# Attention loop of a sandwich layer: a third probability buffer, semaphores per pair of exps, and P·V moved three tiles behind Q·K

## What is computed

```python
q = (x @ Wq + bq).reshape(b, t, H, hd).transpose(0, 2, 1, 3)          # H = 16 heads of 64
k = ((x @ Wk + bk) @ Wl + bl).reshape(b, t, H, lhd).transpose(0, 2, 1, 3)
v = ((x @ Wv + bv) @ Wl + bl).reshape(b, t, H, lhd).transpose(0, 2, 1, 3)
attn = softmax(einsum('bhqd,bhkd->bhqk', q, k) / sqrt(hd))
out = einsum('bhqk,bhkd->bhqd', attn, v)
```

## Time and profile before

| | us |
|---|---|
| median of 2 runs | 4394.33 (4388.55 to 4400.11) |
| the profiled execution | 4391.0 |
| its span on the slowest core (core 2) | 4389.4 |
| spans of all cores | 4366.3 to 4389.4 |
| PE busy, mean granted clock | 2287.8 (52%), 0.762 |
| DVE busy | 1556.0 (35%) |
| ACT busy | 1307.2 (30%) |

### The profile page before, as it was taken

One profiled execution on the slowest core, in us unless ns is written; L12 is line 12 of the kernel. 1 busy time (PEld: TensorE's weight loads), 2 busy tenths in 40 slices (PEclk: granted clock), 3 DMA queues, 4 the chain that ended last, 5 costly groups with the idle time before them and its releaser, 6 DMA issues.

```text
span 4389.4 us, 33357 instructions; the slowest of 8 cores (4366.3 to 4389.4 us)
## 1 busy us (share of the span) xinstructions
PE 2287.8 (52%) x9208; PEld 781.5 (18%) x9296; DVE 1556.0 (35%) x2228; ACT 1307.2 (30%) x1117; POOL 10.1 (0%) x16
## 2 busy tenths in 40 slices
PE   3777555655555554777655555556553333233333
PEld 1333111111111111333211111111111121111121
DVE  2444222232223223444222322222232544555445
ACT  0000355554554550000255454555551000000000
POOL 0000000000000000000000000000000000000000
PEclk9888777877777776888877777778776665566666
DMA  6000100000000002000100000000003112222121
GB/s 116 20 20 1 20 0 0 20 0 20 1 0 20 0 0 77 20 20 1 20 1 1 20 0 0 20 0 20 1 0 82 60 75 96 96 96 88 67 95 58
DMA packets 52842, 137.04 MB, mean 31 GB/s; under 512 B 7479, under 2 KB 7614, under 8 KB 52670
## 3 DMA queue, kind: packets, MB, share of 16 engines
q1 hardware_dynamic: 42206, 117.59, 7.7%
q0 software_dynamic: 10464, 17.32, 2.7%
HBM read 101.87 MB, written 50.33 MB: 35 GB/s over the span
## 4 chain that ended last, share of the span: by engine, by line
PE 34%; DVE 26%; ACT 23%; issue 8%; DMA 5%; DVEq 3%; ACTq 1%; SPq 1%; another core or an unknown queue 0%; POOL 0%; POOLq 0%
ACT pt_sb L434 22%; PE ps L323 13%; DVE xn_fm L468 10%; PE ps L448 3%; PE ps L853 3%; PE ps L508 3%; PE ps L474 3%; PE ps L451 2%; DMA xst<-z_scr 2%; DVEq L165 2%; PE ps L417 1%; DVE xn_tok L487 1%; DVE xn_fm L465 1%; DVE u_s L489 1%; DVE k_sb L885 1%
## 5 line engine op out<-in xcount | busy, mean ns | idle before, releaser
L434 ACT ACTIVATE pt_sb<-ps,cst_sb 128x1024 bf16<-128x1024 f32 x512 | 616.1, 1203 | 984.4 <-PE ps L421 911.1
L448 PE MATMUL ps<-pt_sb,vt_sb 128*65 128x512 bf16 x1024 | 437.0, 427 | 516.1 <-ACTq L165 429.6
L434 ACT ACTIVATE pt_sb<-psT,cst_sb 128x1024 bf16<-128x1024 f32 x512 | 616.1, 1203 | 121.7 <-issue 95.9
L465 DVE COPY xn_fm<-ps 1x512 f32<-1x512 f32 x64 | 43.8, 685 | 1511.1 <-PE ps L451 1511.1
L451 PE MATMUL ps<-pt_sb,vt_sb 128*65 128x512 bf16 x1024 | 437.6, 427 | 0.0
L468 DVE RECIPROCAL xn_fm<-xn_fm 1x1024 f32<-1x1024 f32 x64 | 418.6, 6541 | 5.1
L474 PE MATMUL ps<-xn_fm,ones_sb 1*64 1x512 f32 x128 | 123.8, 1068 | 524.2 <-DVEq L165 524.2
L323 PE MATMUL ps<-xn_fm,arena 128*128 128x512 bf16 x1504 | 349.6, 392 | 30.1 <-DMA blrow_bf<-blrow 15.6
L448 PEld LDWEIGHTS ps<-pt_sb,vt_sb 128*65 128x65 bf16 x1024 | 115.5, 113 | 869.3 <-issue 869.3
L417 PE MATMUL ps<-q_sb,k_sb 64*128 64x512 bf16 x512 | 232.1, 453 | 45.3 <-DMA arena<-wo 38.3
L421 PE MATMUL ps<-q_sb,k_sb 64*128 64x512 bf16 x512 | 232.3, 454 | 0.0
(11 more groups left out here) (137 smaller groups left out, 2214.7 us busy)
## 6 DMA issues: line engine op xcount, KB each, us to landing
xst<-x SPq DMA_DIRECT2D x32, 512.0 KB, 7.6
z_scr<-xst SPq DMA_DIRECT2D x64, 256.0 KB, 3.9
xst<-z_scr SPq DMA_DIRECT2D x64, 256.0 KB, 6.0
k_sb<-x SPq DMA_DIRECT2D x32, 512.0 KB, 8.4
x_scr<-q_sb SPq DMA_DIRECT2D x32, 512.0 KB, 2.6
k_sb<-x_scr SPq DMA_DIRECT2D x32, 512.0 KB, 5.5
out<-q_sb SPq DMA_DIRECT2D x32, 512.0 KB, 2.9
arena<-wq POOLq DMA_DIRECT2D x2, 2048.0 KB, 23.1
```

The lines of the kernel that those rows point to most:

```text
L434: return sc.activation(ptflat[:, pk, :], stb[pk][:, 0:1024], AF.Exp, bias=cst[:, 1:2], scale=cst[:, 0:1])
L448: t.matmul(avA[0:65, :], vt_sb[:, tkc, j, 0:65], pt_sb[:, pk, 0, :], start=(tkc == 0), stop=(tkc == 15))
```

## The change

`pt_sb` gets a third buffer, and exp(t) writes buffer t mod 3, so that it waits for AV(t-3) in place of AV(t-2). ACT's semaphore is raised only after odd exps; whatever waits for exp(t) with t even and is appended after exp(t+1) waits for the value of exp(t+1). AV(t) is appended three tiles behind QK, and ahead of QK(t+3). The two copies of the sums become one of 1 x 1024.

```diff
-        pt_sb = sb("pt_sb", [128, 2, 2, SLT], BF16)
+        pt_sb = sb("pt_sb", [128, 3, 2, SLT], BF16)
...
                     def emit_qk(tkc):
                         pk = tkc % 2
-                        we = exp_done.get((j, tkc - 2)) if tkc >= 2 else \
-                            exp_done.get((j - 1, 14 + tkc) if j > 0 else (7, 14 + tkc))
+                        pp = tkc % 3
+                        wk_ = (j, tkc - 2) if tkc >= 2 else \
+                            ((j - 1, 14 + tkc) if j > 0 else (7, 14 + tkc))
+                        we = exp_done.get(wk_)
+                        if we is None and wk_ in exp_done:
+                            we = exp_done.get((wk_[0], wk_[1] + 1))
...
-                        wav = av_done.get((j, tkc - 2)) if tkc >= 2 else \
-                            av_done.get((j - 1, 14 + tkc) if j > 0 else (7, 14 + tkc))
-                        def fexp(sc, tkc=tkc, pk=pk, qk=qk_done, wav=wav):
+                        wav = av_done.get((j, tkc - 3)) if tkc >= 3 else \
+                            av_done.get((j - 1, 13 + tkc) if j > 0 else (7, 13 + tkc))
+                        def fexp(sc, tkc=tkc, pk=pk, pp=pp, qk=qk_done, wav=wav):
...
-                        exp_done[(j, tkc)] = inc("S", sS)
+                        if tkc % 2 == 1 or tkc == 15:
+                            exp_done[(j, tkc)] = inc("S", sS)
+                            exp_done[(j, tkc - 1)] = exp_done[(j, tkc)]
+                        else:
+                            exp_done[(j, tkc)] = None
...
                     def emit_av(tkc):
-                        pk = tkc % 2
+                        pp = tkc % 3
+                        ed = exp_done[(j, tkc)] or exp_done.get((j, tkc + 1))
...
-                    for tkc in range(17):
+                    AVLAG = 3
+                    for tkc in range(16 + AVLAG):
+                        if tkc >= AVLAG:
+                            emit_av(tkc - AVLAG)
                         if tkc < 16:
                             emit_qk(tkc)
-                        if tkc >= 1:
-                            emit_av(tkc - 1)
...
-                        v.tensor_copy(den_sb[0:1, 0:512], avA[64:65, :])
-                        v.tensor_copy(den_sb[0:1, 512:1024], avB[64:65, :])
+                        v.tensor_copy(den_sb[0:1, :], av2[64:65, :])
```

More of the change, by code:

```diff
@@ L101, in build_nc @@
         vt_sb = sb("vt_sb", [128, 16, 8, 130], BF16)
-        pt_sb = sb("pt_sb", [128, 2, 2, SLT], BF16)
-        pth = pt_sb.bitcast(F32).reshape([128, 1024])
+        pt_sb = sb("pt_sb", [128, 3, 2, SLT], BF16)
+        pth = pt_sb.bitcast(F32).reshape([128, 1536])
         dummy = pth[:, 0:1024]
@@ L138, in build_nc @@
         xn3_tok = ur[:, 2048:4096].rearrange("p (t d) -> p t d", t=2)
-        hs_brhs = pt_sb.reshape([128, 2048])[:, 0:SLT]
+        hs_brhs = pt_sb.reshape([128, 3072])[:, 0:SLT]
         lg_sb = xth[0:6, 0:512]
@@ L393, in emit_phase_B @@
             stb = [ps1[:, 0:1024], psTf[:, 0:1024]]
-            avb = [ps2[:, 0:512], ps2[:, 512:1024]]
+            av2 = ps2[:, 0:1024]
             drb = [ps2[:, 1024:1536], ps2[:, 1536:2048]]
-            ptflat = pt_sb.reshape([128, 2, 1024])
+            ptflat = pt_sb.reshape([128, 3, 1024])
             exp_done = {}
@@ L404, in emit_phase_B @@
                     par = j % 2
-                    avA, avB = avb
+                    avA, avB = av2[:, 0:512], av2[:, 512:1024]
                     def emit_qk(tkc):
                         pk = tkc % 2
-                        we = exp_done.get((j, tkc - 2)) if tkc >= 2 else \
-                            exp_done.get((j - 1, 14 + tkc) if j > 0 else (7, 14 + tkc))
+                        pp = tkc % 3
[4 more added lines that the diff above has]
+                            we = exp_done.get((wk_[0], wk_[1] + 1))
                         def fqk(t, j=j, tkc=tkc, qb=qb, pk=pk, we=we,
@@ L433, in fexp @@
                                 sc.wait_ge(sT.h, wav)
-                            return sc.activation(ptflat[:, pk, :], stb[pk][:, 0:1024],
+                            return sc.activation(ptflat[:, pp, :], stb[pk][:, 0:1024],
                                                  AF.Exp, bias=cst[:, 1:2],
@@ L437, in emit_qk, with fav @@
                         Q["S"].append(fexp)
-                        exp_done[(j, tkc)] = inc("S", sS)
+                        if tkc % 2 == 1 or tkc == 15:
[3 more added lines that the diff above has]
+                            exp_done[(j, tkc)] = None
                     def emit_av(tkc):
-                        pk = tkc % 2
+                        pp = tkc % 3
+                        ed = exp_done[(j, tkc)] or exp_done.get((j, tkc + 1))
                         wat = attn_done.get(j - 1 if j >= 1 else 7)
-                        def fav(t, j=j, tkc=tkc, pk=pk, ed=exp_done[(j, tkc)],
+                        def fav(t, j=j, tkc=tkc, pp=pp, ed=ed,
                                 avA=avA, avB=avB, wat=wat):
@@ L448, in fav @@
                             t.matmul(avA[0:65, :], vt_sb[:, tkc, j, 0:65],
-                                     pt_sb[:, pk, 0, :],
+                                     pt_sb[:, pp, 0, :],
                                      start=(tkc == 0), stop=(tkc == 15))
                             return t.matmul(avB[0:65, :], vt_sb[:, tkc, j, 65:130],
-                                            pt_sb[:, pk, 1, :],
+                                            pt_sb[:, pp, 1, :],
                                             start=(tkc == 0), stop=(tkc == 15))
@@ L455, in emit_av, with fden @@
                         av_done[(j, tkc)] = inc("T", sT)
-                    for tkc in range(17):
+                    AVLAG = 3
+                    for tkc in range(16 + AVLAG):
+                        if tkc >= AVLAG:
+                            emit_av(tkc - AVLAG)
                         if tkc < 16:
                             emit_qk(tkc)
-                        if tkc >= 1:
-                            emit_av(tkc - 1)
-                    def fden(v, avA=avA, avB=avB, ad=av_done[(j, 15)]):
+                    def fden(v, av2=av2, ad=av_done[(j, 15)]):
                         v.wait_ge(sT.h, ad)
-                        v.tensor_copy(den_sb[0:1, 0:512], avA[64:65, :])
-                        v.tensor_copy(den_sb[0:1, 512:1024], avB[64:65, :])
+                        v.tensor_copy(den_sb[0:1, :], av2[64:65, :])
                         v.drain()
```

## The result

The changed kernel takes 4734.20 us (median of 11 runs, 4696.61 to 4806.45) against 4394.53 us (10 runs, 4387.36 to 4447.61) for the kernel before. The ratio is 1.0759, with a 95% interval of 1.0712 to 1.0806: on 4394.5 us that is about +334 us (7.6% slower). Ratios leave out executions in which one die was disturbed, which the medians contain, so the two can differ a little. The profiled execution took 4691.1 us and is the fastest of the changed kernel, so its rows show somewhat less than the mean loss.

What follows compares the result with a forecast made beforehand. No engine was busy throughout; ACT's exps set the pace over most of a block, and between blocks everything waited. 64 blocks at +4.10 us, 262 us, on 4391.0 gave 4653, plus 3 for the median: 4656 us, range 4525 to 4778.

Steps and rivals of the forecast that it cites:

- Sign and mechanism: Phase B: QK(2i+2) waits for exp(2i+1), so ACT and PE take turns once per pair; slower, chance 0.92.
- The period of a pair: Inside a block, two exps with their turn: 3.11 us at 2.4 GHz, 3.65 at 1.2, against 2.82 before.
- g: Gap between a pair's two exps on ACT, without a drain: taken as 0 us, in place of 0.21.
- The block's length: 16 exps of a block, 23.42 us before: 27.96 wholly at 1.2 GHz, or 25.26 if the clock rises early.
- early rise: TensorE's clock rises some 6 us after a block's first exp, two of seven pairs slow: +2.30 us per block, 147 us.
- rival C: Clock rises early, one slow pair, g = -0.08: +1.20 us per block, 77 us, 4471 us; chance 0.05.
- The tail: Block's end: two AVs, not one, behind exp(15), +0.52 us at 2.4 GHz or +1.42 at 1.2; single copy -0.06.
- the middle of the two ends: Per block, 4.10 us between 2.30 (early rise) and 5.90 (wholly at 1.2 GHz), times 64: 262 us.
- rival A: TensorE stays at 1.2 GHz through nearly every block: 5.90 us per block, 378 us, 4772 us; chance 0.28.
- the middle case: Whole kernel, some blocks rising halfway and others not: +4.10 us per block, 4656 us; chance 0.42.
- B: Rival: the clock rises as early in a block as before the change: 147 us, 4541 us; chance 0.22.
- D: Rival: the pair's semaphore does not bind, QK released before the odd exp ends: -134 us, 4260 us; chance 0.03.

Runs made afterwards that it cites:

- first experiment: The changed kernel with one part undone, every exp raising ACT's semaphore again (three buffers, lag of three and single copy stay): 4334.16 us, ratio 0.9875.
- filler kernel: The changed kernel plus one unused 512-column matmul after each odd AV of a block but the last, seven per block: 4529.52 us, ratio 1.0226.

## Why the prediction held, point by point

**Sign and mechanism.** QK(2i+2) waits for exp(2i+1), and ACT and PE take turns once per pair. The profile shows it as forecast: PE's wait moved from AV to QK, and the gaps inside and between pairs are 0.33 and 0.93 at 1.2 GHz (forecast 0.3 and 0.9), and 0.71 between pairs at 2.4 GHz (0.7). ACT's pauses between blocks, the fall of the mean clock below 0.76 and the unchanged phases A and C came as forecast too. Undoing the signal alone (0.9875) and doing it alone (1.1732) show that it is the cause.

**The period of a pair.** Forecast 3.65 at 1.2 GHz, measured 3.67. At 2.4 GHz forecast 3.11 with g = 0 and 3.03 as the lower end, measured 3.01. The gap g was mis-sized: it is -0.10, close to the overlap of DVE's two copies, not 0. The rule of the Trainium skill ("ScalarE: Activation LUTs", § What ACT_TABLE_LOAD costs), an overlap of about 93 ns, agrees with this. I had set against it the rule of the Trainium skill for VectorE ("VectorE: DVE Perf Modes", § The DRAIN you can't avoid), that a semaphore after each copy costs nothing extra, and concluded that g would then stay 0.21. That conclusion was wrong, because the gap of 0.21 is not the semaphore's but the separate drain's: with a semaphore raised by each exp itself, exps start 1.09 apart, as close as the 1.10 of a pair without one.

**The block's length.** At 1.2 GHz throughout 27.96 was forecast, and the rows of such blocks show 27.9 to 28.3. With an early rise 25.26 was forecast, and the block at 0.88 took 24.00; there the clock rose after one slow pair, not two, and g was -0.10. That is the block of rival C (24.16), and my count of two was rounded up: by my own numbers 2.41 + 3.65 = 6.06 us are over after one slow pair, and I had the rise at some 6 us.

**The tail.** Forecast +1.42 and +0.52, with -0.06 for the copy; the pause grew by 12.84 - 11.62 = 1.22 and by 11.98 - 11.62 = 0.36. Sizes about right, but the cause was put in the wrong place: the extra AV at the end comes from the pair's signal, not from the lag (first experiment). The copy itself: 932.23 - 930.93 = 1.30 from its start to the reciprocal, forecast 1.31:

```profile
930.93 1.22 DVE L475 COPY xn_fm<-ps 1x1024 f32<-1x1024 f32 x1 [28.50 <-PE ps L460]
932.23 6.54 DVE L477 RECIPROCAL xn_fm<-xn_fm 1x1024 f32<-1x1024 f32 x1
```

**The step that was off: how often the clock rises.** "I take the middle of the two ends, 4.10 per block" gave 262 us; measured were about 334 (by the ratio), or 5.2 per block, nearer to rival A's 5.90 than to the middle. The middle was a hedge between two ends and not a derivation: 43 of the 64 blocks never left 1.2 GHz, and seven rose early. In the profiled execution the block grew by 27.42 - 23.37 = 4.05 us, where the middle of 4.54 and 1.84 is 3.19. The pauses, those after a projection included, grew by 0.80 per block, where the middle was 0.91. So the miss is in the block's length, that is in the clock. The measured time lies inside the range, between the middle case and A. As cases for the whole kernel, rivals B, C and D are out. B's time of 4541 and C's of 4471 stand on both sides of what the filler kernel gave (1.0226 on 4394.5 is about 4494), in which the clock rose early in every block.

**What the lag does at 1.2 GHz.** I wrote that putting QK(2) ahead of AV(0) spares ACT 0.92 but that the new wait takes it back. For the changed kernel that is right. I did not see that with a signal per exp it would be a gain of 1.2%, which the first experiment shows.

## What to carry to other kernels

Before merging signals, list for each waiter which instruction it truly needs: a consumer of the merged signal waits for the last of the group, and if it feeds the same engine again through a double buffer, the two engines take turns. If the cost is the drain in front of a semaphore, raise the semaphore on the instruction itself: here that gave 1.09 in place of 1.41 us per exp and cost nobody a wait. And a small idle time on TensorE can cost more than itself: here the larger part of the loss was the clock, so price such a wait at both clock levels and look at what the engine does ahead of the rise. Where the rows do not say which level will hold, as here, give both ends and say that the middle is a guess.

## What was not expected of the hardware

- Blocks with PE busy for 22.2 of 28.0 us ran at 1.2 GHz from end to end (43 of 64), while the kernel before stayed at 2.4 GHz with PE busy for 8.66 of 14.10 us. The busy share alone does not say which clock holds. With seven more matmuls per block, in the filler kernel, the clock averaged 0.81 to 0.93 over a block.
- The same block did not always get the same clock: on one core of the changed kernel, with the same instructions behind the same pause of 12.84 us, most blocks stayed at 0.50, and the one at 725.88 rose to 2.4 GHz after its first slow pair. What decides it was not found.
- A drain costs more than the gap it shows: 0.21 in the row, 0.32 in the pace of exps.
- Within one execution of the changed kernel the cores, which all do the same work, differed by 2%, and those with a lower mean clock took longer: 4756.6 us at 0.621 against 4659.4 us at 0.651.
